# A graph layer with attention, mixing and routed experts on one core: earlier zeros, late stores from ScalarE, paired register loads, and other sets of tiles at the tail

## Chip, cores and metric

One Trainium2 chip, one core. The metric is the device time of one execution in microseconds (us), the median of several runs.

## What is computed

`x` has 6250 nodes of 256 features; there are 200,000 edges, sorted by destination. The layer normalizes `x`, adds a graph attention (4 heads) and a mixing block to it, normalizes again, and sends each node to 2 of 8 experts (256 to 512 to 256 features).

```python
xn = _layernorm(x, axis=-1)
x = x + gnn(xn, edge_index) + mix(xn[None])[0]

# the expert part, of the normalized sum
logits = jnp.einsum('bsd,de->bse', xn, Wr) + br
top_vals, top_idx = jax.lax.top_k(logits, K)
w = jax.nn.softmax(top_vals, axis=-1)
for e in range(E):
    h = jax.nn.gelu(jnp.einsum('bsd,dh->bsh', xn, W1[e]) + b1[e], approximate=False)
    y_e = jnp.einsum('bsh,hd->bsd', h, W2[e]) + b2[e]
    y = y + y_e * w_full[..., e, None]
```

## The kernel before

The nodes are 49 tiles of 128 rows (tile 48 has 106). Almost all of the time is one software pipeline of 209 numbered steps, written out by Python loops: at step s each engine runs what the plan gives it for s, in the order of its own loop, and engines meet only at semaphores. SyncE (SP) issues DMAs and counts c = s - 5, so what it does "at c" belongs to the other engines' step c.

- **Edge steps 0 to 168.** GpSimd (POOL) gathers the rows of 1024 edges in 8 indirect DMAs (L1548), VectorE (DVE) weighs them, TensorE (PE) adds them up by destination (`sums`, L2338). Tiles become complete from 48 down to 0.
- **Routing of a tile** starts at the step `route_at[t]`: normalize, choose 2 experts, count. Tiles 48 to 24 are scattered to their places in `sent_dram` by POOL. Tiles 23 to 0 are sorted by expert on PE (`sort`, steps +6 and +7), written to `sorted_dram` (`keep_sorted`, c +8, L1411), and handed out: for each of the 8 experts one DMA copies a window of 128 rows to its place in `sent_dram` (`hand_out`, L1424, pieces of two experts, from SP). The tiles in RUSHED get half of their windows from SP and half from ScalarE (ACT, `hand_out_rest`, L2194, step +10). Tile 1 is routed at 169 and tile 0 at 170, so that their windows go out at 178 and 179.
- **Sets and blocks.** `CUTS = (24, 10, 4)` makes four sets: tiles 48 to 24, 23 to 10, 9 to 4, 3 to 0. When a set's last tile is routed, `table` (DVE) lays its rows out in blocks of 128 rows of one expert: 42, 28, 27 and 15 blocks. One block is a job of one step: load (`block_inputs`, c = job - 3, L1379), turn (PE at job - 1), first matmul (`up`, L2379, at job), gelu (ACT at job + 1), turn (job + 2), second matmul (`down`, L2415, job + 3), `result` (DVE at job + 4, L1786) into one of two buffers `ys`, `store` (SP at c = job + 4, L1388). `result` of a job waits until the store of the job two before has landed. Jobs: set 0 at 82 to 123, set 1 at 124 to 151, set 2 at 155 to 181, set 3 at 183 to 197.
- **Zeros.** The windows leave rows past a set's end unwritten. For sets 2 and 3 (CLOSED) `fills` (SP, L1445) writes a window of 128 zero rows for each expert at the set's end, after the windows of the set's last tile but one; the windows of the last tile wait for the zeros (`fills_out`, L1418 and L2188 in `hand_out` and `hand_out_rest`). For set 3 that is at c = 179.
- **Last part.** For each tile `collect` (POOL, L1570, two indirect DMAs) fetches its two expert rows, `combine` (DVE, L1973 and L1976) weighs and adds them, `give` (SP, L1459) stores them. 45 tiles (sets 0 to 2) come first, three in a step from step 187 on, and their collects wait until the last two blocks of set 2 are stored; the 4 tiles of set 3 come last and wait for the last block of set 3.

```python
# order inside one step s of SyncE (c = s - LAG), cut
block_inputs of job c + 3;  store of the mix job c - 3;  store of the block job c - 4
mixed_again, keep_x1;  fills;  keep_sorted;  hand_out pieces;  x1_again;  give
# order inside one step s of ScalarE, cut
take_x(job s + 1);  take_h(job s - 2);  gelu(job s - 1)
take_tile;  take_sorted;  hand_out_rest;  exponentials
```

Of the kernel before, what the change touches and what calls it, by code (L numbers as in the profile page):

```python
# [37 lines left out]
CUTS = (24, 10, 4)  # L38
# [16 lines left out]
def gps_layer(nc, x, xT, src_cols, dst_cols, W_turned, att_cols, src, dst, gnn_W, att_src, att_dst, gnn_bias, w_qkv, b_qkv, kln_g, kln_b, vln_g, vln_b,  # L55
# [33 lines left out]
    zero_dram = nc.dram_tensor("zero_dram", (P, D), F32).ap()  # L89
# [16 lines left out]
    NS = NG - COUNTED  # L106
    PARTS = EG // PART
# [54 lines left out]
    handed_at = {t: c for c, gone in piece_at_step.items() for t, _ in gone}  # L162
    ups_dram = nc.dram_tensor("ups_dram", (3 * NE, H), BF16).ap()
# [67 lines left out]
    with ExitStack() as ctx:  # L231
# [854 lines left out]
        def loop_stage(ph):  # L1086
# [50 lines left out]
            fill_row = sb("fill_row", [1, NE], I32, c=ph)  # L1137
# [170 lines left out]
            def on_sync(sp):  # L1308
# [52 lines left out]
                def block_inputs(n, x, k):  # L1361
                    b, u = first_block[x] + k, n % 2
                    sp.wait_ge(table_ready, 3 * (x + 1))
# [49 lines left out]
                def hand_out(t, k):  # L1413
# [24 lines left out]
                def fills(x):  # L1438
                    sp.wait_ge(table_ready, 3 * (x + 1))
# [21 lines left out]
                with sp.If(general_value(sp) == 0):  # L1461
# [7 lines left out]
                    for s in range(STEPS + LAG):  # L1469
# [6 lines left out]
                        if s == LAG:  # L1476
                            sp.wait_ge(consts_ready, 4)
                            sp.dma_start(zero_dram, hid[:, 0:D]).then_inc(zero_out, 16)
                        for b in range(SPARE_F):
                            if s == LAG + 3 + b:  # L1480
                                sp.wait_ge(zero_out, 16)
                                sp.dma_start(sent_dram[NE * REGION + b * P:NE * REGION + (b + 1) * P], zero_dram).then_inc(spare_out, 16)
                        for v in range(SORT_BUFS):
                            if s == LAG + 3 + SPARE_F + v:
                                sp.dma_start(sorted_dram[v, 2 * P:3 * P], zero_dram).then_inc(tails_out, 16)
# [11 lines left out]
                        if job and job[1] == "block":  # L1497
# [15 lines left out]
                        for x in CLOSED:  # L1513
                            if max(table_at[x], handed_at[SETS[x][1] + 1] + 1) == c:
# [70 lines left out]
            def on_vector(dve):  # L1585
# [157 lines left out]
                def hidden_bias(n, t):  # L1743
# [4 lines left out]
                    else:  # L1748
                        dve.wait_ge(zero_out, 16)
# [137 lines left out]
                def table(x):  # L1887
                    nb, b0 = set_blocks[x], first_block[x]
                    if filled_by(x - 1):
                        dve.wait_ge(fills_out, filled_by(x - 1))  # L1890
# [23 lines left out]
                    dve.tensor_tensor(fill_row[:], pos[0:1], region[0:1], ALU.add).then_inc(table_ready, 1)  # L1914
# [213 lines left out]
            def on_scalar(act):  # L2128
# [54 lines left out]
                def hand_out_rest(t, k):  # L2183
# [3 lines left out]
                    if filled_by(x if t == SETS[x][1] else x - 1):  # L2187
                        act.wait_ge(fills_out, filled_by(x if t == SETS[x][1] else x - 1))  # L2188
# [7 lines left out]
                def take_sorted(half, t):  # L2196
# [6 lines left out]
                    act.activation(sorted_home[n % 2][:, 0 if half == "low" else 1], ps_xT[:, KT * P:2 * KT * P], ACT.Copy).then_inc(xT_taken, 1)  # L2203

# [1516 lines left out]
```

## Time and profile before

| what | value |
|---|---|
| median of 3 runs | 2163.92 us (2162.31 to 2164.34) |
| the profiled execution | 2166.88 us, its span 2165.1 us |
| TensorE busy / mean granted clock | 1819.3 us (84%) / 0.904 |
| VectorE, ScalarE, GpSimd busy | 1602.0, 1084.9, 1459.0 us |
| DMA | 402.19 MB, mean 186 GB/s |

Spans and starts are counted from the first instruction of the profiled execution; lines (L) are those of the kernel before. "PEld" is the weight load of TensorE, "SPq" and "ACTq" are the DMA issues of SyncE and ScalarE. An idle time before a row names what ended it. The clock is a share of full speed.

### The profile page before, as it was taken

How to read it: one execution, taken by the hardware profiler on the slowest of the kernel's cores; microseconds unless marked ns; L12 is line 12 of the kernel's file. 1: busy time of each engine (PE TensorE's matmuls, PEld its weight loads, DVE VectorE, ACT ScalarE, POOL GpSimd, SP SyncE). 2: the span in 40 equal slices, each digit the busy share in tenths (PEclk: the TensorE clock that was granted, in tenths of full speed). 3: DMA queues.
4: the chain of work that ended last, by engine and by line, in shares of the span. 5: the costliest groups of instructions: out<-in, count | busy, mean ns of one | idle time of the engine just before them, and what ended most of it. 6: DMA issues, size and time to landing. Idle time of an engine off the chain costs nothing. (4 is left out here: it accounts for less than half of the span.)

```text
span 2165.1 us, 37614 instructions
## 1 busy us (share of the span) xinstructions
PE 1819.3 (84%) x9074; PEld 1326.3 (61%) x9075; DVE 1602.0 (74%) x3942; ACT 1084.9 (50%) x1932; POOL 1459.0 (67%) x1586
## 2 busy tenths in 40 slices
PE   8499998688677787767989999989999989997871
PEld 6367776566565565555666667667767767754540
DVE  7678887567777777789888878879868989731243
ACT  4433333235555555446667667667557767532210
POOL 3377777777777777777767777667777777600476
PEclk9799999888777777878999999999999999999995
DMA  9666665776666666656677677667778777522485
GB/s 331 148 188 180 170 175 146 243 235 187 172 181 174 179 175 184 177 158 180 191 206 207 197 212 214 192 180 193 194 197 207 214 200 187 156 69 76 148 247 161
DMA packets 287067, 402.19 MB, mean 186 GB/s; under 512 B 108915, under 2 KB 209555, under 8 KB 283262
## 3 DMA queue, kind: packets, MB, share of 16 engines
q0 software_dynamic: 74208, 206.08, 35.3%
q1 hardware_dynamic: 197036, 180.03, 27.9%
q10 hardware_dynamic: 15602, 13.59, 2.1%
q8 instruction: 83, 1.36, 0.3%
q14 instruction: 138, 1.13, 0.2%
HBM read 346.38 MB, written 82.48 MB: 198 GB/s over the span
## 5 line engine op out<-in xcount | busy, mean ns | idle before, releaser
L1548 POOL DMA_INDIRECT rows_g<-node_table,src_all x1347 | 1285.5, 954 | 478.0 <-issue 404.2
L2338 PE MATMUL psB<-rows_g,pick_e 128*128 128x260 f32 x2704 | 731.8, 431 | 128.3 <-issue 118.5
L2338 PEld LDWEIGHTS psB<-rows_g,pick_e 128*128 128x128 f32 x2704 | 573.4, 218 | 243.8 <-issue 143.5
L1723 DVE TENSOR_TENSOR rows_g<-rows_g,psD 128x2048 f32<-128x2048 f32 x169 | 384.9, 2277 | 0.0
L2136 ACT ACTIVATE pick_n<-local_row 128x1024 bf16<-128x1024 bf16 x169 | 178.6, 1057 | 228.0 <-PE psA L2327 218.4
L2379 PE MATMUL psC<-W_f,xnT 128*128 x448 | 225.5, 626 | 0.0
L1570 POOL DMA_INDIRECT rows_g<-set_dram,places x98 | 96.7, 987 | 168.0 <-issue 163.7
L1694 DVE TENSOR_TENSOR pick_e<-psD,slot_all 128x1024 f32<-128x1024 f32 x169 | 203.7, 1205 | 0.1
L2132 ACT ACTIVATE local_row<-local_row,minus_id 128x1024 bf16<-128x1024 bf16 x169 | 191.5, 1133 | 13.9 <-DVE both_f L2036 8.7
L1786 DVE COPY xn<-psD 128x256 f32<-128x256 f32 x112 | 47.2, 422 | 178.3 <-PE psD L2415 75.2
L2327 PEld LDWEIGHTS psA<-window,pick_n 128*128 128x128 bf16 x1352 | 54.9, 99 | 142.5 <-issue 137.8
L2327 PE MATMUL psA<-window,pick_n 128*128 128x24 bf16 x1352 | 59.5, 174 | 92.6 <-DVE psD L1704 48.3
L1712 DVE TENSOR_TENSOR p_both_e<-rows_g,psD 128x64 f32<-128x64 f32 x169 | 48.9, 289 | 107.8 <-DMA rows_g<-node_table,src_all 101.5
L2379 PEld LDWEIGHTS psC<-W_f,xnT 128*128 128x128 f32 x448 | 77.1, 192 | 81.0 <-issue 81.0
L2415 PE MATMUL psD<-W_f,hidT 128*128 x448 | 117.0, 406 | 0.0
L2415 PE MATMUL psD<-W_f,hidT_more 128*128 x448 | 114.9, 401 | 0.0
L2180 ACT ACTIVATE xdT<-psA 128x256 f32<-128x256 f32 (+1 forms) x49 | 18.8, 383 | 188.8 <-PE psA L2424 186.2
L2142 ACT ACTIVATE xnT<-psA 128x256 f32<-128x256 f32 x112 | 41.9, 374 | 139.6 <-PE psA L2348 131.7
L2415 PEld LDWEIGHTS psD<-W_f,hidT 128*128 128x128 f32 x448 | 83.9, 197 | 16.9 <-issue 0.7
L2463 PE MATMUL psC<-W_f,xnT 128*128 128x512 f32 (+1 forms) x196 | 90.0, 602 | 3.7 <-DMA xnT<-in_xT_dram 3.7
L2415 PEld LDWEIGHTS psD<-W_f,hidT_more 128*128 128x128 f32 x448 | 82.6, 194 | 16.5 <-issue 0.4
L2388 PE MATMUL psC<-ident,hid 128*128 128x128 f32 (+1 forms) x546 | 90.3, 282 | 0.0
(389 smaller groups left out, 3013.1 us busy)
## 6 DMA issues: line engine op xcount, KB each, us to landing
local_row<-local_dram SPq DMA_DIRECT2D x169, 256.0 KB
sent_dram<-sorted_dram SPq DMA_DIRECT2D x176, 128.0 KB
rows_g<-node_table,src_all POOLq DMA_INDIRECT x1347
xin<-sent_dram SPq DMA_DIRECT2D x112, 128.0 KB
set_dram<-xn SPq DMA_DIRECT2D x112, 128.0 KB
xnT<-in_xT_dram SPq DMA_DIRECT2D x96, 128.0 KB
acc<-node_table SPq DMA_DIRECT2D x49, 128.0 KB
W_f<-in_x_dram SPq DMA_DIRECT2D x48, 128.0 KB
```

The costliest lines, as they stand in the source:

```text
L1548: pool.indirect_dma_start(out=rows_g[:, r, j], out_offset=None, in_=node_table, in_offset=bass.IndirectOffsetOnAxis(ap=src_all[:, g, j:j + ...
L1570: pool.indirect_dma_start(out=final_home(f)[0][0:rows, c], out_offset=None, in_=set_dram[span_of[x]], in_offset=bass.IndirectOffsetOnAxis( ...
L1694: dve.tensor_tensor(pick_e[:, r], ids_here.unsqueeze(1).broadcast_to([P, EG, P]), slot_all[:, g].unsqueeze(2).broadcast_to([P, EG, P]), AL ...
L1723: dve.tensor_tensor(heads, heads, p_here.unsqueeze(3).broadcast_to([P, EG, HEADS, C]), ALU.mult).then_inc(ph_ready, 1)
L2132: act.activation(local_row[:, r], local_row[:, r], ACT.Abs, bias=minus_id[:]).then_inc(away_ready, 1)
L2136: act.activation(pick_n[:], local_row[:, r], ACT.Relu, bias=1.0, scale=-1.0).then_inc(pick_n_ready, 1)
L2327: last = pe.matmul(ps_pick[:, j * 6 * HEADS:(j + 1) * 6 * HEADS], pick_n[:, j * P:(j + 1) * P], window[:, w].rearrange("p k a -> p (k a)") ...
L2338: last = pe.matmul(ps_sum[s % 2][:, 0:AW], pick_e[:, s % SLOTS, j], rows_g[:, s % RING, j, 0:AW], start=(j == 0), stop=(j == EG - 1))
L2379: last = pe.matmul(ps_up[:, :], xnT[:, u, c], W1_f[:, bass.ds(e, 1), c], start=False, stop=(c == KT - 1))
L2388: last = pe.transpose(ps_hT[:, c * P:c * P + rows], hid[0:rows, c * P:(c + 1) * P], ident[0:rows, 0:rows])
L2415: last = pe.matmul(ps_small[:, down_at], turned_rows(n, kind)[:, c], W2_f[:, bass.ds(e, 1), c], start=False, stop=(c == HK - 1))
L2463: last = pe.matmul((ps_up, ps_hT)[u][0:rows, :], xnT[:, u, k, 0:rows], wkv_s[:, k], start=(k == 0), stop=(k == KT - 1))
```

## The change

- `CUTS` (24, 10, 5): set 2 is tiles 9 to 5 (25 blocks), set 3 is tiles 4 to 0 (17 blocks). The plan's steps become: jobs of set 2 at 152 to 176 (no step without a job between sets 1 and 2), of set 3 at 183 to 199; `table` of set 2 at 142 in place of 148; the first 44 tiles are collected from step 182 on, five last tiles at 204 and 205; 211 steps. `route_at` is unchanged. In RUSHED tile 5 takes the place of tile 4.
- `fills` comes before the windows of the set's last two tiles: for set 2 at c = 137 (149 before), for set 3 at 176 (179 before). It writes 3 x 128 zero rows for each expert, at the places where the last tile but one begins, from `cuts` in place of `fill_row`; the windows of both last tiles wait for it. `table` no longer waits for zeros.
- `store` of block jobs from job 169 on is issued by ScalarE, at the end of its step job + 5, in place of SyncE.
- `hand_out` and `fills` load several register values with one load.

```diff
-CUTS = (24, 10, 4)
+CUTS = (24, 10, 5)
...
-    zero_dram = nc.dram_tensor("zero_dram", (P, D), F32).ap()
+    zero_dram = nc.dram_tensor("zero_dram", (3 * P, D), F32).ap()
...
+    LATE = NS
...
+    fill_at = {x: max(route_at[SETS[x][1] + 1] + 7, handed_at[SETS[x][1] + 2] + 1) for x in CLOSED}
...
 def hand_out(t, k):
...
-                    if filled_by(x if t == SETS[x][1] else x - 1):
-                        sp.wait_ge(fills_out, filled_by(x if t == SETS[x][1] else x - 1))
+                    if filled_by(x if t <= SETS[x][1] + 1 else x - 1):
+                        sp.wait_ge(fills_out, filled_by(x if t <= SETS[x][1] + 1 else x - 1))
...
-                    for e in range(BY_TWO * k, BY_TWO * (k + 1)):
-                        frm = sp.value_load(cuts[0:1, n % SORT_BUFS, 0, e:e + 1], min_val=0, max_val=2 * P)
-                        to = sp.value_load(cuts[0:1, n % SORT_BUFS, 1, e:e + 1], min_val=0, max_val=NE * REGION - P)
-                        sp.dma_start(sent_dram[bass.ds(to, P)], sorted_dram[n % SORT_BUFS, bass.ds(frm, P)]).then_inc(handed[k], 16)
+                    two = slice(BY_TWO * k, BY_TWO * (k + 1))
+                    _, frm = nc.values_load_multi_w_load_instructions(cuts[0:1, n % SORT_BUFS, 0, two], engines=[mybir.EngineType.SP], min_val=0, max_val=2 * P)
+                    _, to = nc.values_load_multi_w_load_instructions(cuts[0:1, n % SORT_BUFS, 1, two], engines=[mybir.EngineType.SP], min_val=0, max_val=NE * REGION - P)
+                    for e in range(BY_TWO):
+                        sp.dma_start(sent_dram[bass.ds(to[e], P)], sorted_dram[n % SORT_BUFS, bass.ds(frm[e], P)]).then_inc(handed[k], 16)
...
 def fills(x):
-                    sp.wait_ge(table_ready, 3 * (x + 1))
-                    if x:
-                        for k in range(HANDS):
-                            sp.wait_ge(handed[k], handed_by(SETS[x][1] + 1))
-                    for e in range(NE):
-                        at = sp.value_load(fill_row[0:1, e:e + 1], min_val=0, max_val=NE * REGION - P)
-                        sp.dma_start(sent_dram[bass.ds(at, P)], zero_dram).then_inc(fills_out, 16)
+                    t = SETS[x][1] + 1
+                    n = sort_number(t)
+                    sp.wait_ge(cuts_ready, 2 * (n + 1))
+                    for k in range(HANDS):
+                        sp.wait_ge(handed[k], handed_by(t + 1))
+                    for e in range(0, NE, 4):
+                        _, to = nc.values_load_multi_w_load_instructions(cuts[0:1, n % SORT_BUFS, 1, e:e + 4], engines=[mybir.EngineType.SP], min_val=0,
+                                                                         max_val=NE * REGION - 3 * P)
+                        for at in to:
+                            sp.dma_start(sent_dram[bass.ds(at, 3 * P)], zero_dram).then_inc(fills_out, 16)
...
-                        if job and job[1] == "block":
+                        if job and job[1] == "block" and c - 4 < LATE:
                             store(*job)
...
-                            if max(table_at[x], handed_at[SETS[x][1] + 1] + 1) == c:
+                            if fill_at[x] == c:
                                 fills(x)
...
 def table(x):
-                    if filled_by(x - 1):
-                        dve.wait_ge(fills_out, filled_by(x - 1))
...
+                def store(n, kind, a, k):
+                    act.wait_ge(ys_ready, n + 1)
+                    act.dma_start(set_dram[span_of[a]][(set_at[a] + k) * P:(set_at[a] + k + 1) * P], ys[:, n % 2]).then_inc(ys_out[n % 2], 16)
...
+                        if s - 5 >= LATE and jobs_with(s - 5):
+                            store(*jobs_with(s - 5))
```

Where instructions stand now. First, ScalarE around its windows of tiles 1 and 0 (L2194 before, L2198 now; the windows of tile 1 come ahead). Before, from the last window of tile 1 to the first of tile 0:

```order
L2194 DMA sent_dram<-sorted_dram 16x2048
L2142 ACTIVATE xnT<-psA 128x256
L2159 ACTIVATE hidT<-psC 128x512
L2152 ACTIVATE hid<-psC 128x512
L2192 TENSOR_LOAD cuts
L2192 ISA x2
```

Now, ScalarE from the last window of tile 1, with the store of job 174 behind it:

```order
L2198 DMA sent_dram<-sorted_dram 16x2048
L2211 DMA set_dram<-xn 128x256
L2196 TENSOR_LOAD cuts
L2196 ISA x2
L2197 TENSOR_LOAD cuts
```

And ScalarE now from the last window of tile 0 to the first work of set 3's blocks:

```order
L2198 DMA sent_dram<-sorted_dram 16x2048
L2211 DMA set_dram<-xn 128x256 x2
L2146 ACTIVATE xnT<-psA 128x256 x3
L2156 ACTIVATE hid<-psC 128x512
L2146 ACTIVATE xnT<-psA 128x256
```

The copies and the gelu of jobs (L2142, L2159, L2152) that stood between the windows are gone from there; the stores of jobs 174, 175 and 176 stand between and behind them, and the next job's work comes after.

Second, SyncE at the zeros of set 3. Before, from the last window of tile 1 that SyncE issues to the zeros (their 8 loads and DMAs stand one after the other, and the windows of tile 0 follow them):

```order
L1424 DMA sent_dram<-sorted_dram 16x2048
L1388 DMA set_dram<-xn 128x256
L1444 TENSOR_LOAD fill_row
L1444 ISA x2
L1445 ISA
L1445 DMA sent_dram<-zero_dram 16x2048
```

Now, SyncE from the load of job 176 to the zeros:

```order
L1381 DMA xin<-sent_dram 128x256
L1448 TENSOR_LOAD cuts
L1448 ISA x8
L1451 ISA
L1451 DMA sent_dram<-zero_dram 16x6144
```

And SyncE now from the last zeros to the windows of tile 1:

```order
L1451 DMA sent_dram<-zero_dram 16x6144
L1413 DMA sorted_dram<-w_s 128x2x256
L1413 DMA sorted_dram<-weff 128x2x256
L1424 TENSOR_LOAD cuts
L1424 ISA x4
L1425 TENSOR_LOAD cuts
L1425 ISA x4
L1427 ISA
```

The zeros stand ahead of both tiles' sorted rows and windows, right behind a load of set 2, and no load or store of a job stands between them and the windows any more.

## Rows read from the trace of the kernel before

**Rows 1.** Page, part 5, GpSimd's gathers (count, busy us, mean ns, idle before).

```profile
L1548 POOL DMA_INDIRECT rows_g<-node_table,src_all x1347 | 1285.5, 954 | 478.0 <-issue 404.2
...
L1570 POOL DMA_INDIRECT rows_g<-set_dram,places x98 | 96.7, 987 | 168.0 <-issue 163.7
```

**Rows 2.** Timeline, GpSimd at the end (start us, length us, operation).

```profile
2028.18 1.58 POOL L1570 DMA_INDIRECT rows_g<-set_dram,places  x1 [137.56 <-issue]
...
2154.42 0.94 POOL L1570 DMA_INDIRECT rows_g<-set_dram,places  x1 [0.30 <-issue]
```

**Rows 3.** Timeline, VectorE: the last tile's second sum.

```profile
2157.74 0.48 DVE L1976 SCALAR_TENSOR_TENSOR rows_g<-rows_g,share 128x256 f32<-128x256 f32 x1
```

**Rows 4.** Timeline, ScalarE and its DMA queue, 1960 to 2010 us.

```profile
1967.46 0.60 ACT L2152 ACTIVATE hid<-psC 128x512 f32<-128x512 f32 x1
...
1977.92 6.26 ACTq L2194 DMA_DIRECT2D sent_dram<-sorted_dram  x4
...
1999.98 6.23 ACTq L2194 DMA_DIRECT2D sent_dram<-sorted_dram  x4
2006.32 0.60 ACT L2159 ACTIVATE hidT_more<-psC 128x512 f32<-128x512 f32 x1 [20.67 <-DMA sent_dram<-sorted_dram]
```

**Rows 5.** Timeline, SyncE's DMA issues, 1930 to 2130 us.

```profile
1936.15 0.34 SPq L1379 DMA_DIRECT2D xin<-sent_dram  x1
...
1972.08 0.39 SPq L1411 DMA_DIRECT2D sorted_dram<-weff  x1
1974.30 6.52 SPq L1424 DMA_DIRECT2D sent_dram<-sorted_dram  x4
...
1986.92 9.78 SPq L1445 DMA_DIRECT2D sent_dram<-zero_dram  x8
...
2008.85 0.36 SPq L1379 DMA_DIRECT2D xin<-sent_dram  x1
...
2025.11 0.43 SPq L1388 DMA_DIRECT2D set_dram<-xn  x1
...
2126.29 0.33 SPq L1388 DMA_DIRECT2D set_dram<-xn  x1
```

**Rows 6.** Timeline, VectorE: cut places of tile 1, results of two blocks.

```profile
1943.38 0.16 DVE L1870 CAST cuts<-acc 1x8 int32<-1x8 f32 x1
...
2022.13 0.42 DVE L1786 COPY xn<-psD 128x256 f32<-128x256 f32 x1 [4.16 <-PE psD L2415]
2031.48 0.42 DVE L1786 COPY xn<-psD 128x256 f32<-128x256 f32 x1 [8.93 <-PE psD L2415]
```

**Rows 7.** Chain of waits, edge steps with blocks (start, length, what).

```profile
1823.12 3.51 PE psB L2338 x16
...
1833.68 3.51 PE psB L2338 x16
```

**Rows 8.** Timeline, TensorE: second matmuls of three blocks.

```profile
2044.51 1.99 PE L2415 MATMUL psD<-W_f,hidT_more 128*128 x8
...
2049.53 1.99 PE L2415 MATMUL psD<-W_f,hidT 128*128 x8
...
2073.58 3.52 PE L2415 MATMUL psD<-W_f,hidT 128*128 x8
```

**Rows 9.** Chain of waits at the end: DMAs, issue to landing.

```profile
1996.18 2.36 DMA sent_dram<-zero_dram
...
2055.65 3.40 DMA set_dram<-xn
...
2111.20 2.21 DMA set_dram<-xn
```

**Rows 10.** Stretches: busy us by engine, granted clock, DMA share, GB/s.

```profile
1975.00:2010.00 35.00, 15.83 (x59) 9.04 (x58) 0.85 (x2) 3.92 (x8) 0.00 (x0) 0.78 0.31 95
2060.00:2110.00 50.00, 36.94 (x128) 21.87 (x126) 21.16 (x47) 9.20 (x19) 38.09 (x40) 0.90 0.81 247
2110.00:2130.00 20.00, 7.78 (x18) 5.14 (x18) 9.24 (x21) 0.00 (x0) 15.12 (x17) 0.61 0.70 211
```

More of the change, by code:

```diff
@@ L162, in gps_layer @@
     handed_at = {t: c for c, gone in piece_at_step.items() for t, _ in gone}
+    fill_at = {x: max(route_at[SETS[x][1] + 1] + 7, handed_at[SETS[x][1] + 2] + 1) for x in CLOSED}
+    assert all(fill_at[x] < min(c for c, gone in piece_at_step.items() if SETS[x][1] + 1 in dict(gone)) for x in CLOSED)
     ups_dram = nc.dram_tensor("ups_dram", (3 * NE, H), BF16).ap()
@@ L1136, in loop_stage @@
             blk_expert = sb("blk_expert", [1, P], I32, c=ph)
-            fill_row = sb("fill_row", [1, NE], I32, c=ph)
             cuts = sb("cuts", [1, SORT_BUFS, 2, NE], I32, c=ph)
@@ L1362, in block_inputs @@
                     b, u = first_block[x] + k, n % 2
-                    sp.wait_ge(table_ready, 3 * (x + 1))
+                    sp.wait_ge(table_ready, 2 * (x + 1))
                     at = sp.value_load(blk_row[0:1, b:b + 1], min_val=0, max_val=NE * REGION // P + SPARE_F - 1)
@@ L1477, in on_sync @@
                             sp.wait_ge(consts_ready, 4)
-                            sp.dma_start(zero_dram, hid[:, 0:D]).then_inc(zero_out, 16)
+                            for k in range(3):
+                                sp.dma_start(zero_dram[k * P:(k + 1) * P], hid[:, 0:D]).then_inc(zero_out, 16)
                         for b in range(SPARE_F):
                             if s == LAG + 3 + b:
-                                sp.wait_ge(zero_out, 16)
-                                sp.dma_start(sent_dram[NE * REGION + b * P:NE * REGION + (b + 1) * P], zero_dram).then_inc(spare_out, 16)
+                                sp.wait_ge(zero_out, 48)
+                                sp.dma_start(sent_dram[NE * REGION + b * P:NE * REGION + (b + 1) * P], zero_dram[0:P]).then_inc(spare_out, 16)
                         for v in range(SORT_BUFS):
                             if s == LAG + 3 + SPARE_F + v:
-                                sp.dma_start(sorted_dram[v, 2 * P:3 * P], zero_dram).then_inc(tails_out, 16)
+                                sp.dma_start(sorted_dram[v, 2 * P:3 * P], zero_dram[0:P]).then_inc(tails_out, 16)
                         c = s - LAG
@@ L1748, in hidden_bias @@
                     else:
-                        dve.wait_ge(zero_out, 16)
+                        dve.wait_ge(zero_out, 48)
                     dve.scalar_tensor_tensor(out=hid[0:rows, 0:D], in0=ps_up[0:rows, 0:D], scalar=rstd_x[0:rows, t:t + 1], in1=beff[0:rows],
@@ L1913, in table @@
                     dve.tensor_tensor(blk_row[:, b0:b0 + nb], blk_f[:, 1, 0:nb], numbers, ALU.add).then_inc(table_ready, 1)
-                    dve.tensor_tensor(fill_row[:], pos[0:1], region[0:1], ALU.add).then_inc(table_ready, 1)
                     then(dve.tensor_tensor(blk_end[:], blk_end[:], blocks[:], ALU.subtract))
@@ L2186, in hand_out_rest @@
                     act.wait_ge(sorted_out[n % 2], 16 * (n // 2 + 1))
-                    if filled_by(x if t == SETS[x][1] else x - 1):
-                        act.wait_ge(fills_out, filled_by(x if t == SETS[x][1] else x - 1))
+                    if filled_by(x if t <= SETS[x][1] + 1 else x - 1):
+                        act.wait_ge(fills_out, filled_by(x if t <= SETS[x][1] + 1 else x - 1))
                     if n >= 1:
@@ L2354, in expert_of @@
                     b = first_block[a] + k
-                    pe.wait_ge(table_ready, 3 * (a + 1))
+                    pe.wait_ge(table_ready, 2 * (a + 1))
                     experts[n] = pe.value_load(blk_expert[0:1, b:b + 1], min_val=0, max_val=NE - 1)
```

1 line of the change is left out of this document (removed).

## The prediction, made before the changed kernel ran

> **What bounds the kernel now.** I read the page first, then the timelines of GpSimd, ScalarE and SyncE backwards from the end, and last the edge steps. All times are from the span's start.
>
> The last 127 us belong to GpSimd. It starts the first collect at 2028.18 and ends the last at 2154.42 + 0.94 = 2155.36 [rows 2]: 98 collects in 127.2 us, 1.298 each, of which 0.99 is work [rows 1], with no longer pause between them. The last tile's second sum ends at 2158.22 [rows 3], 2.9 after the last collect; the store and the end of the program take the span to 2165.1, 9.7 behind the last collect. So the end is the first collect's start + 127.2 + 9.7, and the blocks of set 3 don't count: their last store starts at 2126.29 [rows 5], when GpSimd still has four tiles of other sets to fetch.
>
> Why does the first collect start only at 2028? It waits for the store of set 2's last block, issued at 2025.11 [rows 5]; its result stood at 2022.13 [rows 6]. That block is late because blocks of set 2 share ScalarE with the windows of tiles 1 and 0. ScalarE waits 20.67 us in one place for the windows of tile 0 [rows 4], and these wait for the zeros: tile 1's windows go out at 1974.30 (SyncE) and 1977.92 (ScalarE) [rows 4, 5], the zeros from 1986.92 on [rows 5], the last of them lands 2.36 after its issue at 1996.18 [rows 9], tile 0's windows follow at 1999.98 [rows 4], and set 3's first load at 2008.85 [rows 5]. TensorE is busy 15.83 of these 35 us, and the DMA engines 31% of them [rows 10]. Gelus and turns of set 2's last four blocks stand in ScalarE's queue between and behind those windows.
>
> **What the change does, part by part.**
>
> *Edge steps.* Three blocks (jobs 152 to 154 are now taken) move into edge steps from behind them. A step with a block takes 10.56 us, TensorE's work end to end (1823.12 to 1833.68) [rows 7]; without one it can't be under the gathers, 8 x (0.954 + 404.2 / 1347) = 10.03 [rows 1]. That is 3 x 0.53 = 1.6. Bounds: 0, and 3 x 5.02 = 15.1 if TensorE pays each block in full (5.02 is the period of blocks alone, 2044.51 to 2049.53 [rows 8]). Set 2's zeros are three times as many bytes, beside gathers; with them I take **+2**, nearest to the gathers' row, since the gathers are the step's other limit.
>
> *Steps 169 to 176* keep a block in each step, so the routing of tiles 1 and 0 stays where it was. What ends there is set 2: five blocks fewer are left, and nothing of them stands behind the windows except second matmuls, results and stores.
>
> *Zeros.* They need only the cut places of tile 1 (1943.38 + 0.16 [rows 6]) and the windows of tile 2. SyncE has issued the load of job 176 at 1936.15 [rows 5] and has no load or store left, so the zeros start at about 1943.6. They are 8 x 384 KB = 3.15 MB. Lower bound: in the stretch of 35 us the engines moved 95 GB/s at a share of 0.31 [rows 10], 306 GB/s if always busy, so 10.3 us, landed by 1956. Upper: three times what the 8 small ones took, 9.78 + 2.36 = 12.1 [rows 5, 9], 36.4 us, by 1980. I take the lower end and a few us, 1956 to 1960, because the small ones were paced by their issue. Either way they are off the path until ScalarE's windows of tile 1 could start.
>
> *ScalarE's windows.* It ends block 176's gelu at 1967.46 + 0.60 = 1968.06 [rows 4]. One more copy of sorted rows, one of turned hidden rows and two stores (0.43 each on SyncE [rows 5]) bring it to 1970.1. Tile 1's windows: 6.26 [rows 4], to 1976.4. Store of 174: 0.45. Tile 0's windows: 6.23, to 1983.1; their sorted rows are written by then, since SyncE no longer waits for a turn of TensorE as it did before 1972.08 [rows 5]. Two stores: 0.9, to 1984.0; landing 3 (3.40 and 2.21 [rows 9]): 1987. With the 2 us of the edges **the first collect starts at 1989**, 39 earlier. Set 3's first load follows tile 0's last window as before (2008.85 - 2006.21 = 2.64) [rows 4, 5]: 1985.7 + 2 = 1988.
>
> *Stores on ScalarE.* A store now stands behind the gelu of a later block, so `result` can wait for the store of the block two before. In the last steps of set 2 this moves results by some 3 us, inside the times above. In set 3 a step takes GpSimd's 7.8 us (three tiles, six collects), and the store lands in time. SyncE loses its stores; nobody waits for them there. I cost it at nothing until GpSimd's pace is gone.
>
> *Paired loads* shorten SyncE's windows (6.52 for four [rows 5]) by two loads a pair; ScalarE's four, unchanged, end later, so: 0. `table` loses a wait that has long been met and one small operation: 0.
>
> *Last part.* First collect 1989. 44 tiles, 88 x 1.298 = 114.2: 2103.2. Do the blocks of set 3 hold GpSimd up? From the first load to the first result took 22.6 us (2008.85 to 2031.48 [rows 5, 6]), with set 2's rest between them: 2011 here. That result is wanted by VectorE ahead of the tenth tile's sums, whose rows land at 1989 + 26 + 3 = 2018. They don't. The 44th tile's sums end 2.9 after its collect, at 2106.1; by VectorE's order the result of job 195 stands right behind them: 2106.5. Four more blocks (196 to 199) have nothing to hide behind: 4 x 5.02 = 20.1, less 3 x 1.99 [rows 8] for first matmuls already done, plus 2.3 for a result that waits for the store of two blocks before (that store stands behind block 199's gelu): 16.4. TensorE's clock in the stretch of the collects is 0.90 [rows 10]; at the low level (1.2 GHz) a group of eight takes 3.52 in place of 1.99 [rows 8], so five groups cost 7.7 more, and at 0.90 a fifth of that, 1.5. Job 199's result: 2124.5. Its store: 3.3, 2127.8. Ten collects with their start, 13.3: 2141.1. The end: 9.7.
>
> **Sum:** span 2150.8 against 2165.1, -14.3. The profiled execution took 2166.88, 2.96 over the median of 2163.92; the new median is 2163.92 - 14.3 = **2149.5**, -0.7%. 39 us are won at the first collect; 25 go back because five blocks and ten collects now stand one behind the other.
>
> **Rivals.**
>
> *The low clock at the end.* TensorE, paced by GpSimd, is busy 36.94 of 50 us at a clock of 0.90 (2060 to 2110), and 7.78 of 20 at 0.61 (2110 to 2130) [rows 10]: it falls when gaps grow. If the last five blocks fall into such a time, 7.7 - 1.5 = 6.2 more: 2155.7. Against: the four blocks are denser than what comes ahead. The Trainium skill (TensorE: Matmul & The Clock Gate, HAM oscillation — how this bites in real kernels) says that gaps in which the engine waits for DMAs return it to the throttled level, each time anew. The trace agrees for the stretch at 0.61, not for the one at 0.90; by that rule the time would be this rival's.
>
> *The edges pay in full*, 15.1 in place of 2: 2162.6, no change. For it: steps around the relocation of places (VectorE) are long and the old plan had its empty steps near them. Against: in the trace each long step is followed by a short one.
>
> *The early start does not come*: if GpSimd starts where it did, it needs 127.2 + 9.7 as before, 2164. Nothing found that would hold it there.
>
> *The zeros land late: slower.* If the eight DMAs ran one behind the other, each three times 2.36 [rows 9], they would take 56.6 us, to 2000. ScalarE's windows of tile 1 would start 30 later than 1970.1, and everything after: 2180. From 1970 on each us of the zeros costs one; it turns slower when they land after 1984.5, 41 us for 3.15 MB. For it: no row shows so large a copy within DRAM. Against: the share of 0.31 [rows 10]. The Trainium skill (DMA: Bandwidth & Descriptors, Queues, rings and completion order) says that a semaphore's increment lands only after all earlier writes of that DMA engine, across its queues. By that rule the stores of blocks 170 to 172 would also come behind late zeros, which delays ScalarE's path again by some 9 us, 2189; no run here shows it yet.
>
> **How the numbers follow.** Forecast 0.64; low clock 0.13; edges in full 0.09; no early start 0.06; zeros late 0.08. The 80% range takes in the forecast with its bounds (edges at 0, full clock, no wait for a store, stores landing in 2.21: 9 less), the low clock, and the edges in full: 2140 to 2163. A measurement can tell 0.2%, 4.3 us: faster is below 2159.6, slower above 2168.2. Faster 0.77; same 0.15; slower 0.08.
>
> **What would show it.** Right: the first collect near 1989; ScalarE's eight windows near 1970 to 1983 with no wait of 20 us; zeros landed before 1970; a hole in the collects of some 25 us before the last ten. Wrong: the zeros' last landing after 1970, results of set 2 that wait for stores by more than 3 us, a last sum of edges later than 2 us, or GpSimd pausing among the first 88.

## The result and the profile after

The changed kernel takes **2148.20 us** (median of 4 runs, 2147.61 to 2148.67) against 2164.13 in the same comparison (4 runs, 2162.31 to 2167.90): ratio 0.9930, 95% interval 0.9917 to 0.9942. Forecast were 2149.5 and 2140 to 2163. The span of the profiled execution went from 2165.1 to 2145.6, -19.5, where the sum had -14.3.

GpSimd at the end of the changed kernel, in its timeline (start us, length us, engine, line, operation, idle time before it and what ended that):

```profile
1990.36 1.58 POOL L1577 DMA_INDIRECT rows_g<-set_dram,places  x1 [99.21 <-issue]
...
2103.66 0.95 POOL L1577 DMA_INDIRECT rows_g<-set_dram,places  x1 [0.30 <-issue]
2123.60 0.94 POOL L1577 DMA_INDIRECT rows_g<-set_dram,places  x1 [18.99 <-issue]
...
2134.85 0.95 POOL L1577 DMA_INDIRECT rows_g<-set_dram,places  x1 [0.30 <-issue]
```

The idle time before the first collect is the stretch from the last gather of the edges to the first collect: 99.2 us, where it was 137.6 [rows 2]. Then 88 collects run without a pause (1990.36 to 2104.61, 1.298 each), a hole of 19 us opens that was not there before, ten more follow, and the span ends 9.8 behind the last of them. From the first collect to the end it is now 155.2 us, where it was 136.9 (2165.1 - 2028.18). So 38.4 us are won ahead of the first collect, 18.3 are given back behind it, and the gathers ended 0.5 later.

ScalarE's timeline shows why the collects start sooner:

```profile
1967.40 0.60 ACT L2156 ACTIVATE hid<-psC 128x512 f32<-128x512 f32 x1
...
1970.86 6.30 ACTq L2198 DMA_DIRECT2D sent_dram<-sorted_dram  x4
1977.20 0.59 ACTq L2211 DMA_DIRECT2D set_dram<-xn  x1
1979.26 6.24 ACTq L2198 DMA_DIRECT2D sent_dram<-sorted_dram  x4
1985.54 1.37 ACTq L2211 DMA_DIRECT2D set_dram<-xn  x2
```

The windows of tile 1 and tile 0 are 2.1 us apart, with one store between; the wait of 20.67 us [rows 4] is gone. The last store of set 2 leaves right behind them, near 1986.5, and the first collect starts some 4 later. SyncE's issues in the same stretch:

```profile
1936.71 0.35 SPq L1381 DMA_DIRECT2D xin<-sent_dram  x1
1945.66 6.75 SPq L1451 DMA_DIRECT2D sent_dram<-zero_dram  x8
...
1971.42 13.34 SPq L1427 DMA_DIRECT2D sent_dram<-sorted_dram  x8
1988.08 3.25 SPq L1381 DMA_DIRECT2D xin<-sent_dram  x3
```

The zeros leave 41 us sooner than before (1986.92 [rows 5]). Counted from the last gather they leave after 54.5 us; before it was 96.3, and with the early zeros alone 69.9 (zeros_alone below, at 1958.15). So the new place is worth 26 us of it; the rest comes with the emptier queue, in which no load or store of set 2 is left ahead of them. VectorE's results, first of set 2 (blocks 172, 173 and the last, 176), then of set 3 (183, and 195 to 199):

```profile
1958.33 0.42 DVE L1793 COPY xn<-psD 128x256 f32<-128x256 f32 x1 [2.65 <-DMA set_dram<-xn]
1963.71 0.42 DVE L1793 COPY xn<-psD 128x256 f32<-128x256 f32 x1 [0.27 <-DMA set_dram<-xn]
...
1979.78 0.42 DVE L1793 COPY xn<-psD 128x256 f32<-128x256 f32 x1 [8.40 <-DMA set_dram<-xn]
2019.55 0.42 DVE L1793 COPY xn<-psD 128x256 f32<-128x256 f32 x1
...
2107.62 0.42 DVE L1793 COPY xn<-psD 128x256 f32<-128x256 f32 x1
2110.33 0.42 DVE L1793 COPY xn<-psD 128x256 f32<-128x256 f32 x1 [2.29 <-PE psD L2425]
2115.13 0.42 DVE L1793 COPY xn<-psD 128x256 f32<-128x256 f32 x1 [4.38 <-PE psD L2425]
2117.85 0.42 DVE L1793 COPY xn<-psD 128x256 f32<-128x256 f32 x1 [2.30 <-PE psD L2425]
2120.58 0.42 DVE L1793 COPY xn<-psD 128x256 f32<-128x256 f32 x1 [2.30 <-PE psD L2425]
```

Most of the hole is the last four of these rows: blocks 196 to 199 come behind the 44th tile's sums, 12.96 us from 2107.62 to 2120.58. The other 6.0 are those sums ahead (2104.61 to 2107.62) and the last store behind (2120.58 to 2123.60). And block 176 still waited 8.40 for a store that stood behind the windows of tile 1: as a run below shows, the start is not yet as early as it could be.

### The profile page after: what moved, and what is told of

It reads as the page before. It is cut to its first block and busy times, and to the rows that moved or that the text cites. A ratio compares the mean times of both kernels' runs of the same rounds, so it can differ in the third digit from the quotient of the medians.

```text
span 2145.6 us, 37431 instructions
## 1 busy us (share of the span) xinstructions
PE 1811.9 (84%) x9074; PEld 1317.5 (61%) x9075; DVE 1601.7 (75%) x3938; ACT 1085.7 (51%) x1932; POOL 1455.4 (68%) x1586
## 5 line engine op out<-in xcount | busy, mean ns | idle before, releaser
L2348 PE MATMUL psB<-rows_g,pick_e 128*128 128x260 f32 x2704 | 723.6, 427 | 126.0 <-issue 116.3
L2348 PEld LDWEIGHTS psB<-rows_g,pick_e 128*128 128x128 f32 x2704 | 567.1, 215 | 240.3 <-issue 141.9
L1577 POOL DMA_INDIRECT rows_g<-set_dram,places x98 | 96.3, 983 | 148.3 <-issue 143.4
L2337 PEld LDWEIGHTS psA<-window,pick_n 128*128 128x128 bf16 x1352 | 54.8, 99 | 137.6 <-issue 133.3
L2425 PE MATMUL psD<-W_f,hidT_more 128*128 x448 | 121.5, 418 | 0.0
L2425 PEld LDWEIGHTS psD<-W_f,hidT 128*128 128x128 f32 x448 | 81.5, 192 | 15.9 <-issue 0.2
```

Of the source, the lines that this page charges most:

```text
L1577: pool.indirect_dma_start(out=final_home(f)[0][0:rows, c], out_offset=None, in_=set_dram[span_of[x]], in_offset=bass.IndirectOffsetOnAxis( ...
L2337: last = pe.matmul(ps_pick[:, j * 6 * HEADS:(j + 1) * 6 * HEADS], pick_n[:, j * P:(j + 1) * P], window[:, w].rearrange("p k a -> p (k a)") ...
L2348: last = pe.matmul(ps_sum[s % 2][:, 0:AW], pick_e[:, s % SLOTS, j], rows_g[:, s % RING, j, 0:AW], start=(j == 0), stop=(j == EG - 1))
L2425: last = pe.matmul(ps_small[:, down_at], turned_rows(n, kind)[:, c], W2_f[:, bass.ds(e, 1), c], start=False, stop=(c == HK - 1))
```

## Experiments

Two theories for the 38 us. **Theory 1**: the zeros are what counts; the new sets only trade blocks ahead of the collects for blocks behind them; stores and loads give next to nothing. **Theory 2**: the sets are the gain. The table is read with two measures from each trace, which together make up the tail and leave out how long the edges took: the *start*, from the end of the last gather to the first collect (the bracket of that row), and the *rest*, from the first collect to the end of the span. Each comes from one execution. Kernels that differ little show how far that can be trusted: the starts of loads_back and the change, of both and both_paired, and of the change and two_a_step lie 0.1 to 0.7 apart, the rests of loads_back and the change 2.1. The ratio is to the kernel before, timed in the same comparison, with its interval.

| kernel | sets | early zeros | late stores | paired loads | median us | ratio | start | rest |
|---|---|---|---|---|---|---|---|---|
| before | old | | | | 2164.13 | | 137.6 | 136.9 |
| sets_alone | new | | | | 2164.19 | 1.0004 (0.9994 to 1.0014) | 115.3 | 157.1 |
| zeros_alone | old | yes | | | 2152.67 | 0.9955 (0.9938 to 0.9971) | 124.0 | 137.5 |
| late_stores_back | old | yes | | yes | 2156.76 | 0.9959 (0.9944 to 0.9974) | 122.0 | 137.2 |
| sets_back | old | yes | yes | yes | 2166.16 | 1.0004 (0.9991 to 1.0017) | 136.7 | 136.4 |
| old_sets_ahead | old | yes | ahead of windows | yes | 2158.07 | 0.9971 (0.9956 to 0.9986) | 129.7 | 136.8 |
| sets_and_stores | new | | yes | | 2162.22 | 0.9992 (0.9983 to 1.0002) | 114.6 | 156.0 |
| stores_back | new | yes | | yes | 2154.63 | 0.9965 (0.9952 to 0.9977) | 103.6 | 155.6 |
| loads_back | new | yes | yes | | 2148.53 | 0.9926 (0.9910 to 0.9943) | 99.1 | 157.3 |
| **the change** | new | yes | yes | yes | 2148.20 | 0.9930 (0.9917 to 0.9942) | 99.2 | 155.2 |
| stores_ahead | new | yes | ahead of windows | yes | 2141.50 | 0.9907 (0.9885 to 0.9929) | 90.4 | 159.3 |
| two_a_step | new | yes | yes | yes | 2130.66 | 0.9842 (0.9825 to 0.9858) | 98.6 | 135.9 |
| both | new | yes | ahead of windows | yes | 2127.36 | 0.9832 (0.9816 to 0.9849) | 90.7 | 139.9 |
| both_paired | new | yes | ahead of windows | ScalarE too | 2125.45 | 0.9819 (0.9805 to 0.9832) | 90.9 | 140.2 |

**sets_back**

```diff
-CUTS = (24, 10, 5)
+CUTS = (24, 10, 4)
```

> The changed kernel with the old sets (24, 10, 4); early zeros, stores from ScalarE and paired loads stay. Theory 1 (what counts is that the windows of the last tile no longer wait 20 us for the zeros; the sets only trade blocks ahead of the collects for blocks behind them): ScalarE's last window near 1985 as in the changed kernel, five more blocks of set 2 behind it, so the first collect about 22 us after it (as before: 2006 to 2028), near 2007; no hole in the collects, since 15 blocks hide behind 90 of them; end 127.2 + 9.7 later: span near 2144, time within 0.2% of the changed kernel's 2148.2. Theory 2 (the sets give the gain: five blocks fewer stand behind the windows): most of the gain is lost, time 2158 or more.

Measured: no gain is left, 2166.16. The first collect starts at 2030.87. By the two expectations Theory 2 has won, but the next two runs say otherwise.

**sets_alone**

```diff
-CUTS = (24, 10, 4)
+CUTS = (24, 10, 5)
```

> The kernel before with the new sets (24, 10, 5) alone; zeros, stores and loads as before. Theory 1: ScalarE still waits some 20 us ahead of the windows of tile 0, the store of the last block of set 2 goes out from SyncE behind its own windows, near 2008; first collect near 2012; then 88 collects (114), the same hole as in the changed kernel (19), ten collects (12) and the end (9.8): span near 2167, time 2168, no gain or 0.2% slower. Theory 2: most of the gain, time 2150 to 2155.

Measured: no gain, as Theory 1 had it. The first collect is sooner than I expected (2004.05), for ScalarE, with no block left to serve, sits in all its eight windows in one piece, and the last store of set 2 needs nothing of it. Tile 1's windows go out from 1968.09 (1977.92 before), so the zeros behind them leave at 1978.41 (1986.92 before) and the last store at 2000.97, where I had 2008. Its timeline:

```profile
1968.09 29.68 ACTq L2194 DMA_DIRECT2D sent_dram<-sorted_dram  x8
```

The sets move the start by 22.3 us and the rest by 20.2 the other way: alone they are a trade at par.

**zeros_alone** (the old table, sets, stores and single loads; `fills` and its waits as in the change)

```diff
 def fills(x):
+    t = SETS[x][1] + 1
+    n = sort_number(t)
...
+        sp.dma_start(sent_dram[bass.ds(at, 3 * P)], zero_dram).then_inc(fills_out, 16)
```

> The kernel before with the early zeros of three times 128 rows alone; old sets, all stores from SyncE, single loads. Theory 1: nearly as the changed kernel with the old sets, some 0 to 5 us later because SyncE's own windows stand ahead of its stores: first collect 2007 to 2012, span 2144 to 2149, time 2146 to 2151, so nearly the whole gain with one part in four. Theory 2: time near 2160, less than a quarter of the gain.

Measured: 2152.67, about two thirds of the gain from one part (0.45% of 0.70%). That is between the two expectations, nearer to Theory 1, which had 2146 to 2151 and nearly the whole gain. The first collect comes at 2012.27, the late end of what Theory 1 expected; the start gains 13.5 and the rest stays.

```profile
2012.27 1.57 POOL L1574 DMA_INDIRECT rows_g<-set_dram,places  x1 [124.02 <-issue]
```

So with the old sets something that came with the zeros in sets_back takes the gain away again: the stores or the loads.

**stores_back**

```diff
-    LATE = NS
+    LATE = 10 ** 6
```

> The changed kernel with all block stores from SyncE again. Theory 1 (as the prediction has it, the stores cost or give next to nothing): the store of the last block of set 2 leaves SyncE behind its own windows near 1985 where ScalarE's left at 1985.5, time within 2 us of 2148.2. Rival: on SyncE the late stores queue behind loads of rows and outputs that wait for collects, results of set 3 then wait for them: the last blocks come 5 to 15 us later, time 2153 to 2163.

Measured: 2154.63, 6.4 slower, and not for the reason of either expectation. Of the 6.8 between the two profiled spans (2152.4 and 2145.6) 4.3 lie in the start, 2.1 in edges that ended later (1893.25 against 1891.15), and 0.4 in the rest, where the rival looked for them. SyncE's issues show it:

```profile
1939.20 19.58 SPq L1390 DMA_DIRECT2D set_dram<-xn  x4
1960.49 6.75 SPq L1451 DMA_DIRECT2D sent_dram<-zero_dram  x8
...
1993.76 0.42 SPq L1390 DMA_DIRECT2D set_dram<-xn  x1
```

SyncE stays with set 2's stores until 1958.8, so the zeros leave 15 us later than in the change (1945.66). The last store stands behind SyncE's own windows and behind set 3's first load (1993.36), which waits for them; it leaves 7 later than ScalarE's. The edges are 2.1 of both numbers.

**loads_back**

```diff
-                    for e in range(BY_TWO):
-                        sp.dma_start(sent_dram[bass.ds(to[e], P)], ...)
+                    for e in range(BY_TWO * k, BY_TWO * (k + 1)):
+                        frm = sp.value_load(cuts[0:1, n % SORT_BUFS, 0, e:e + 1], ...)
```

> The changed kernel with one register value per load again, in the windows and the zeros. Theory (as the prediction has it): SyncE's four windows take 6.5 us where they take about 5.4, nobody on the path waits for them; time within 2 us of 2148.2. Rival: the loads are SyncE's time ahead of set 3's first load or in the edge steps, and give 3 us or more: 2151 and above.

Measured: 2148.53, no difference from the change. The paired loads are worth nothing here.

**late_stores_back** (old sets, stores from SyncE)

```diff
-CUTS = (24, 10, 5)
+CUTS = (24, 10, 4)
-    LATE = NS
+    LATE = 10 ** 6
```

> The changed kernel with the old sets (24, 10, 4) and all block stores from SyncE again; early zeros and paired loads stay. Theory (it was the stores from ScalarE that lost the gain with the old sets, because results of set 2 wait behind its windows): time as with the zeros alone, 2151 to 2155, first collect near 2012. Rival (the paired loads, or something else that came with the zeros): 2160 or more, as with the old sets and ScalarE's stores (2166.2).

Measured: 2156.76, just over the theory's range; its interval overlaps that of zeros_alone. The start is 122.0; the first collect comes at 2017.99, later than the expected 2012, with edges that ended 7.8 later (1896.00 against 1888.25). So it is the stores from ScalarE that lose 14.7 us of start with the old sets. The waits of that stretch, grouped (engine, line, for what: us in total, times, longest), first of sets_back:

```profile
DVE xn L1793 <- DMA set_dram<-xn: 44.8, 7, 13.2
```

and of late_stores_back:

```profile
DVE xn L1793 <- DMA set_dram<-xn: 24.3, 3, 10.8
```

Results of set 2 wait 20 us more for stores. With the new sets the same stores *win* 4.3.

**sets_and_stores**

```diff
-CUTS = (24, 10, 4)
+CUTS = (24, 10, 5)
...
-                        if job and job[1] == "block":
+                        if job and job[1] == "block" and c - 4 < LATE:
...
+                        if s - 5 >= LATE and jobs_with(s - 5):
+                            store(*jobs_with(s - 5))
```

> The kernel before with the new sets and the late stores from ScalarE; zeros late as before, single loads. Theory (the zeros must be early, or nothing of the rest counts): ScalarE waits about 20 us in its windows as with the sets alone, its stores stand behind them, first collect 2003 to 2008, time 2163 to 2168, no gain. Rival (the stores free SyncE, so that the old zeros come soon enough): first collect near 1995, time 2150 to 2155.

Measured: 2162.22, the first collect at 2004.55, as expected: without the early zeros, sets and stores together give nothing that can be told from none.

**two_a_step**

```diff
-COLLECT_RATE = 3
+COLLECT_RATE = 2
```

> The changed kernel with two tiles collected per step in place of three, so that the plan has a block of set 3 for every two tiles: 44 tiles in 22 steps, and the results of all 17 blocks stand before the 44th tile's sums instead of four of them behind it. Theory (the hole of 19 us ahead of the last ten collects is nothing but these blocks in VectorE's order): a block needs 5.02 us where four collects need 5.19, so they hide; hole 0 to 4 us, first collect unchanged near 1990, span 2127 to 2132, time 2130 to 2135. Rival: blocks and collects together do not hold 5.2 us (DMA engines at 0.76 already, first result of set 3 not before 2011): GpSimd pauses among the first 88 instead, time 2140 or more.

Measured: 2130.66, as the theory had it. The hole is gone: 98 collects from 1992.89 to 2119.03 without a pause, and the last result of set 3 stands long before the last of them (VectorE's timeline):

```profile
2091.56 0.42 DVE L1793 COPY xn<-psD 128x256 f32<-128x256 f32 x1
2095.77 0.42 DVE L1793 COPY xn<-psD 128x256 f32<-128x256 f32 x1 [1.65 <-PE psD L2425]
```

**stores_ahead** (ScalarE's late stores stand ahead of its windows in each step; the last block of set 2 is stored a step sooner)

```diff
+                for at in range(LATE, STEPS - 5):
+                    if jobs_with(at):
+                        early = jobs_with(at)[0] == last_job[-2]
+                        store_at.setdefault(at + (4 if early else 5), []).append(jobs_with(at))
...
+                        for m in store_at.get(s, ()):
+                            store(*m)
                         for t in RUSHED:
                             if route_at[t] + 10 == s:
```

> The changed kernel with ScalarE's stores of a step ahead of its windows, and the store of the last block of set 2 one step sooner, ahead of the windows of tile 0. Theory (the first collect waits for that store, and the store for the windows): the result of block 176 no longer waits 8 us for the store of 174, the stores of 175 and 176 leave near 1977 where they left at 1985.5, first collect near 1982, 8 us sooner, time near 2140. Rival: the first result of set 3 can't come sooner, VectorE then holds up GpSimd, and 3 us or less arrive: 2145 or more.

Measured: 2141.50; the start falls by 8.8, the result of block 176 stands at 1972.80 in place of 1979.78, the first collect at 1980.50. The edit has two parts, and counted from the last gather the traces tell them apart: the result of block 176 comes 5.9 sooner (stores ahead of the windows), and from it to the first collect it takes 7.7 in place of 10.6 (the last store, a step sooner). The rest grows by 4 us, for GpSimd now pauses 4.45 once, near 2002, for sums in VectorE's queue. The first of these sums does not come sooner than in the change (1999.87 there):

```profile
1995.01 1.24 SPq L1460 DMA_DIRECT2D rows_g<-x_dram  x3
1999.86 0.48 DVE L1977 SCALAR_TENSOR_TENSOR rows_g<-rows_g,share 106x256 f32<-106x256 f32 x1 [25.47 <-DMA rows_g<-x_dram]
2001.77 0.94 POOL L1577 DMA_INDIRECT rows_g<-set_dram,places  x1 [4.45 <-DVE rows_g L1977]
```

By the second row it waits not for a result of set 3, as the rival had it, but for the tile's own rows that SyncE fetches (`x1_again`), and SyncE issues these behind set 3's first three loads (from 1990.78), which come behind the windows. That points to SyncE's order for the 4 us; no run tried another.

**both**

```diff
-COLLECT_RATE = 3
+COLLECT_RATE = 2
...
+                        for m in store_at.get(s, ()):
+                            store(*m)
```

> Both edits of the two runs before: stores ahead of the windows, and two tiles a step. Theory: the gains add while set 3's blocks keep up: first collect near 1982, 98 collects in 127, end 9.8 later: span 2119, or up to 2126 where the first result of set 3 (not before 2011) holds up the collects; time 2121 to 2129. Rival: blocks of set 3 are the bound from then on, and this is no faster than two tiles a step alone.

Measured: 2127.36 (2122.51 to 2128.50), the fastest kernel up to here, 0.983 of the kernel before. The profiled execution took 2122.51 with a span of 2120.5 and one pause of 3.55 us. The median is only 3.3 under that of two_a_step and the intervals overlap; that the gains add is read from the start and the rest together (4.7 us less than the change for stores_ahead, 19.9 for two_a_step, 23.8 for both), not from the medians alone. Stretches of this kernel (us from and to, length, busy us with count of instructions in brackets of PE, PEld, DVE, ACT, POOL, granted clock, DMA share, GB/s):

```profile
2010.00:2040.00 30.00, 30.00 (x121) 18.10 (x120) 13.25 (x30) 8.81 (x18) 23.00 (x24) 1.00 0.84 257
2040.00:2070.00 30.00, 30.00 (x120) 18.01 (x119) 13.12 (x30) 8.81 (x18) 22.83 (x24) 1.00 0.90 277
```

and of the changed kernel:

```profile
2020.00:2050.00 30.00, 25.41 (x80) 14.61 (x80) 11.96 (x26) 5.88 (x12) 22.72 (x24) 0.81 0.80 237
2050.00:2080.00 30.00, 24.87 (x80) 14.35 (x80) 12.74 (x28) 5.64 (x12) 22.96 (x24) 0.83 0.80 236
```

GpSimd does the same 24 collects in 30 us in both, while TensorE does half as many matmuls again beside them.

**both_paired**

```diff
-                        frm = act.value_load(cuts[0:1, n % SORT_BUFS, 0, e:e + 1], ...)
+                    _, frm = nc.values_load_multi_w_load_instructions(cuts[0:1, n % SORT_BUFS, 0, two], engines=[mybir.EngineType.Activation], ...)
```

> The kernel with stores ahead of the windows and two tiles a step, with paired register loads in ScalarE's windows too. Theory (ScalarE's windows of tiles 1 and 0 are still what set 2's last stores and set 3's first load wait for): four windows take about 5.3 in place of 6.3 us, first collect 1 us and first load of set 3 up to 2 us sooner, time 1 to 2 us below the 2127.4 without, 2125 to 2127. Rival: GpSimd's pace alone sets the end, 2127 to 2128.

Measured: the windows take 5.09 and 5.36 us, as expected, but the start is 90.9 as before (90.7): the windows of tile 1 leave 1.1 us later behind their sorted rows (4.17 after SyncE's issue of these in place of 3.06), which eats the gain. Why they do is open. 2125.45 can't be told from 2127.36.

**old_sets_ahead** (as stores_ahead, with the old sets)

```diff
-CUTS = (24, 10, 5)
+CUTS = (24, 10, 4)
...
+                        for m in store_at.get(s, ()):
+                            store(*m)
```

> The changed kernel with the old sets (24, 10, 4), late stores from ScalarE put ahead of its windows (the last block of set 2 one step sooner too). With the old sets the results of set 2 waited 44.8 us for stores when ScalarE issued these (first collect 136.7 us after the last gather), and 24.3 us when SyncE did (122.0). Theory (the stores lose with the old sets because they stand behind ScalarE's windows): waits for stores fall to 20 us or less, the first collect comes 115 to 124 us after the last gather, no hole, time 2146 to 2156. Rival (a store that leaves ScalarE a step later than it left SyncE is late in every step, windows or not): the first collect stays 130 us or more after the last gather, time 2160 or more.

Measured: between the two, start 129.7. The waits for stores hardly fell, to 42.1 us, so the theory's own sign did not come. The result of set 2's last block tells where the 7.0 us of start come from. In sets_back, late_stores_back and this run:

```profile
2020.74 0.42 DVE L1793 COPY xn<-psD 128x256 f32<-128x256 f32 x1 [4.34 <-DMA set_dram<-xn]
2011.98 0.42 DVE L1793 COPY xn<-psD 128x256 f32<-128x256 f32 x1 [4.16 <-PE psD L2425]
2013.99 0.42 DVE L1793 COPY xn<-psD 128x256 f32<-128x256 f32 x1 [4.27 <-DMA set_dram<-xn]
```

Counted from the last gather it stands at 126.6, 116.0 and 123.3, and the first collect follows it after 10.1, 6.0 and 6.3. So the stores from ScalarE cost 10.6 ahead of that result and 4.1 behind it. Of these 14.7, moving the stores ahead of the windows gives back 3.2, and storing the last block a step sooner 3.8. Part of the rest may lie in another queue: with the old sets SyncE still has loads of set 2 ahead of the zeros, which then leave from 1961 to 1965 on and meet the late stores. The first row is ScalarE's issue of block 172's store, the second the result that waits for it, in sets_back, where the zeros leave from 1965.17 to 1971.91:

```profile
1971.09 0.33 ACTq L2211 DMA_DIRECT2D set_dram<-xn  x1
...
1978.70 0.42 DVE L1793 COPY xn<-psD 128x256 f32<-128x256 f32 x1 [8.81 <-DMA set_dram<-xn]
```

The result could follow that store only after 7.6 us. How the remaining 7.7 divide between this and the step that each store leaves later was not tried by itself and stays open.

## Why the prediction held, and where it did not

- **The bound** was read rightly: GpSimd's 98 collects, and ahead of them the last store of set 2 behind ScalarE's windows. None of the rivals came. For the low clock: TensorE's granted clock was 0.96 where the last blocks stand alone, and each of their groups of eight took 1.99, the length at the high level [rows 8]. First the stretch, then the last group:

```profile
2104.00:2125.00 21.00, 15.50 (x63) 9.69 (x61) 3.97 (x9) 2.77 (x5) 1.70 (x3) 0.96 0.21 68
2118.55 1.99 PE L2425 MATMUL psD<-W_f,hidT 128*128 x8
```

  So the 1.5 us that the sum took for the clock did not come either. The rival at 0.13 stood beside a rule of the Trainium skill (TensorE: Matmul & The Clock Gate, HAM oscillation — how this bites in real kernels), that gaps in which the engine waits for DMAs throttle it. This stretch does not test the rule: between the four blocks TensorE waited 0.52 us at most, and for VectorE's results. Those were what it waited for in the stretch at 0.61 before, too (two waits, 6.7 us).
- **Zeros**: issued 1945.66 to 1952.41 (forecast from 1943.6), landed near 1957.3, inside 1956 to 1960. In the view of DMAs of that stretch (bytes each, median us to landing):

```profile
sent_dram<-zero_dram SPq DMA_DIRECT2D x8, 384.0 KB, 4.9
```

- **ScalarE's windows**: tile 1 at 1970.86 (forecast 1970.1, with the 2 us of the edges 1972.1), tile 0 ended 1985.50 (1985.1), first collect 1990.36 (1989), first load of set 3 at 1988.08 (1988). The last landed within 1.4 us.
- **Edges**: +2 was taken for three more blocks and the larger zeros; the gathers ended 0.5 later (start row: 1990.36 - 99.21, against 2028.18 - 137.56). That is less than executions differ in this part (below), so the term is neither confirmed nor refuted; the 15 us of the rival are refuted.
- **The last four blocks are the step that was mis-sized**: 16.4 + 1.5 were forecast, 12.96 came. The 2.3 for a result that waits for the store of two blocks before did not happen (none of the four rows names a store), nor did the 1.5 for the clock; the last 1.1 is spread over the blocks. The hole was 19 where I wrote some 25, and this is 4.9 of the 5.2 by which the span (2145.6) fell short of 2150.8; the ten collects took 1.1 less than their 13.3 (2123.60 to 2135.80), and the 44 tiles ended about as much later.
- **The median came nearer than the terms, in part by luck.** The span fell by 19.5 between the two profiled executions, the medians by 15.9: the execution profiled before lay 2.75 above its median, the one profiled after 0.59 below. Had the median moved as the spans did, it would be 2144.4, 5 us under the forecast in place of 1.3. The lower bound was also added up too low: the four terms named for it (2, 1.5, 2.3, and 0.8 + 1.1 for two stores) make 7.7, not 9.
- **One of its own signs of being wrong came**: the result of block 176 waited 8.40 for a store, where the prediction had some 3. It cost the forecast nothing, since the store of 176 stood behind tile 0's windows in any case; stores_ahead, which moved both, started 8.8 sooner.
- **"Nobody waits for SyncE's stores"** was wrong, though the sum did not suffer from it: I placed the zeros at 1943.6 because SyncE had nothing left to do, which holds only because the stores had gone to ScalarE. With them back, the zeros leave at 1960.49 and the time is 6.4 longer.
- **The parts.** The prediction said what the whole does and left open which part does it. In the start, sets (22.3) and zeros (13.5, with the loads 15.6) nearly add up to what both give (34.0). The stores add 4.3 to that, next to nothing without the zeros (0.7), and take 14.7 with the old sets. In the rest, the new sets cost 18 to 21 as long as three tiles go in a step, and 22.5 with the stores ahead of the windows, 4.45 of it GpSimd's pause. Of the two theories, then, neither holds alone: without the zeros the other parts give nothing, without the sets the stores undo the zeros.
- **The rival "zeros late"** rested on a rule of the Trainium skill (DMA: Bandwidth & Descriptors, Queues, rings and completion order): an increment lands only after earlier writes of that DMA engine, across queues. It did not come, but a delay that would fit it is seen in small. ScalarE's stores of blocks 170 and 171 in the change:

```profile
1953.67 0.34 ACTq L2211 DMA_DIRECT2D set_dram<-xn  x1
1960.80 0.33 ACTq L2211 DMA_DIRECT2D set_dram<-xn  x1
```

  The first, issued just behind the last zeros, let block 172's result go at 1958.33, 4.7 us later; the second, with the zeros landed, block 173's at 1963.71, 2.9 later. In sets_back it was 7.6 for block 172's store, issued near the end of the zeros' issues. The store of block 171, issued there at their start (1965.17), took less, though the zeros had not landed when its waiter went:

```profile
1965.38 0.34 ACTq L2211 DMA_DIRECT2D set_dram<-xn  x1
...
1969.46 0.42 DVE L1793 COPY xn<-psD 128x256 f32<-128x256 f32 x1 [4.27 <-DMA set_dram<-xn]
```

  The traces agree with the rule: what was issued ahead of the store counts. Sharing of the engines may have a part in it; no run here separates the two.

## What to carry to other kernels

An edit that moves the start of a bound engine forward is worth only what its last inputs leave: ask what the end will then wait for, and give those inputs their place in the order too (here one number, two tiles a step in place of three, was worth more than the whole change). Take a change of several parts apart with single parts added *and* single parts removed: the same stores won 4 us in one setting and lost 15 in another. A queue that runs in program order carries a cost for whatever stands behind, so a moved DMA is counted at both the queue that it joins and the queue that it leaves.

## Not expected of the hardware

- A small store issued late in a large copy, or just behind it, is held up with the copy; one issued at the copy's start is not. From the store's issue to the waiting result it took 4.7, 6.8 and 7.6 us at the end of the issues of 3.15 MB of zeros (the change, old_sets_ahead, sets_back), 4.1 and at most 2.2 at their start (sets_back, old_sets_ahead), 2.9 after their landing (the change).
- The edges end at different times in kernels whose edge part is the same. The last gather ended at 1890.65, 1894.17 and 1896.00 in old_sets_ahead, sets_back and late_stores_back, which differ only in stores from job 169 on, and at 1889.86 to 1894.33 in both, stores_ahead, the change and two_a_step: 5.4 and 4.5 us that lie ahead of everything in which these kernels differ. Single profiles of two kernels are better compared from the last gather on.
- Three more matmuls for every six, beside the same indirect DMAs, did not slow GpSimd's collects, with the DMA engines at 0.84 to 0.90; TensorE's granted clock was 1.00 in that stretch, where it was busy without a gap (30.00 of 30.00 us), and 0.81 to 0.83 in the change, where it was busy 25 of 30.
